# Four transformer layers on one core: where the softmax of the two 32-wide attentions is divided by its row sums

## The chip, the cores and the metric

The kernel runs on one core of one Trainium2 chip. The metric is the device time of one execution in microseconds; lower is better. Engines are named as in the profile: PE is TensorE (PEld its weight loads), DVE VectorE, ACT ScalarE, POOL GpSimd, SP the engine that issues DMAs.

## The reference

Four pre-norm transformer layers follow each other on x of 4 batches x 512 rows x 512 columns, each `x = x + attention(layernorm(x))`, then `x = x + feed_forward(layernorm(x))`. The change touches the attentions of the first two layers, 16 heads 32 wide, causal:

```python

q = (x @ Wq).reshape(B, S, N_KV, GROUP, HEAD_DIM)
k = (x @ Wk).reshape(B, S, N_KV, HEAD_DIM)
v = (x @ Wv).reshape(B, S, N_KV, HEAD_DIM)
scores = jnp.einsum('bqkgd,bskd->bkgqs', q, k) * scale
scores = jnp.where(causal, jnp.finfo(scores.dtype).min, scores)
attn = jax.nn.softmax(scores, axis=-1)
...

AV = jnp.einsum('bhqk,bhkd->bhqd', A, V)
return AV @ Wo + bo
```

The first five lines and the mask are layer 0 (4 key/value heads, each shared by 4 query heads, no biases; the heads go through V and Wo as in layer 1); the last two are layer 1, with 16 key/value heads, its own second layernorm weights ln_g and ln_b, and biases bq, bk, bv, bo. Everything is float32.

## The kernel before

Both attentions are made by one function, `attention32` (line 502), called as a0 (one chunk of keys, `split_y` true) and a1 (four chunks, biased). x stays in SBUF for the whole kernel. A float32 product that needs full precision is made of three (`product`, lines 101 to 103) from high and low halves; one that doesn't is `plain` (line 108).

Work is cut into 16 units an attention: 4 batches b times 4 groups u of 4 heads (128 rows of features). A unit has three chunks j: the scores of query tile 3 (512 wide), of tiles 2 and 0 (384 + 128), of tile 1 (256). For each chunk n:

- S: TensorE makes the scores of four heads into banks 0 to 3, in two halves (line 950).
- `low`: VectorE adds the causal mask, writes P and takes the row minimum (line 867); this frees the score banks.
- `exp`: ScalarE, in place, with the row sums in `total` (line 788).
- `rec`: VectorE takes the inverse of the sums (line 873) and multiplies heads 0 and 1 of P by them (line 878); GpSimd multiplies heads 2 and 3 (line 715).
- PT: TensorE turns 128x128 tiles of P, four to a group, ten groups a unit (line 961), into banks 4 and 5; ScalarE copies each group out (line 795).
- PV: TensorE multiplies by V into bank 6 (line 976). Behind the tenth group ScalarE copies O (line 800), and GpSimd passes it on to OT: in a0 as a high and a low half (lines 735, 737), in a1 as a copy (line 739).

Between these stand "pieces", each into bank 7: projections Q, K, V (VT and V in a0) of this or the next batch, T (transposes of the normalised x for the next batch), Y (the output product of the batch before). A Q or K piece is read by ScalarE (high half) and then VectorE (low half, lines 851, 848); a Y piece is added to x by VectorE (line 895); T is copied by ScalarE, cast by GpSimd (line 708), its low half made by VectorE (line 833).

The order is a list written out by hand, `ORDER`. Every engine walks it and does its own kinds, in that order, so a wait of one engine holds all that stands behind it on that engine. Iteration n has: `low` (n+2, 0 and 1), `rec` (n+1), `low` (n+2, 2 and 3), then two halves, each of up to two PT, the PV of two groups before, two `exp` of chunk n+2, and in the first half the near piece; then the first half of S for chunk n+3, the far piece, the second half of S. Near and far pieces go by (u, j); for j = 1 the near piece is Y for u = 0 and 1, Q for u = 2, and for u = 3 Q in a0 and V in a1; in the first batch there is no Y, in the last no piece of a next batch. For j = 0 the far piece is a K in a1, except for u = 2, where it is a T in both. Banks are handed over by counting semaphores: a job waits until the job before it in its bank has been read.

## Time and profile before

| what | us |
|---|---|
| median of 3 runs | 3340.04 (3339.21 to 3345.2) |
| the profiled execution | 3342.46 |
| its span, first to last instruction | 3340.6 |
| TensorE busy in it | 2978.2 (89%) |
| VectorE busy | 1976.6 (59%) |
| ScalarE busy | 1556.4 (47%) |
| GpSimd busy | 1030.8 (31%) |

The page gives busy time by engine and the costliest groups of instructions. A group's row has the line, the engine, the operation, written tile <- read tiles, shapes and count, then its busy time, the mean duration of one in ns, and the idle time of the engine just before, with what ended it. The names `a_...` cover both attentions here and two later ones; the line tells them apart. Matmuls overlap, so the time that one takes of TensorE is busy time through count, not its mean duration. "PEclk" is the mean clock granted to TensorE, 1.00 for 2.4 GHz and 0.50 for 1.2 GHz.

a0 lies in about the first 376 us, a1 between about 795 and 1245 us. The stretches 36:366 and 803:1232 hold most of them.

### The profile page before, as it was taken

The numbers are of one execution on the slowest core, as the hardware profiler recorded it, in microseconds if no ns is written. First come the engines' busy times: TensorE is split into PE (matmuls) and PEld (weight loads), VectorE is DVE, ScalarE is ACT, GpSimd is POOL, SyncE is SP. The second block draws the span as 40 slices with busy tenths as digits, with TensorE's granted clock in tenths as the row PEclk, the third lists the DMA queues.
The fourth block names the chain that finished last, engine by engine and source line by source line (L and its number), as shares of the span: only waits on it lengthen the run. The fifth ranks groups of instructions, "written<-read, shape, count | busy, mean of one in ns | idle before, by whom it ended". The sixth has DMA issues, their size and how long they took to land. (4 is left out here: it accounts for less than half of the span.)

```text
span 3340.6 us, 46876 instructions
## 1 busy us (share of the span) xinstructions
PE 2978.2 (89%) x16388; PEld 2252.2 (67%) x16388; DVE 1976.6 (59%) x5344; ACT 1556.4 (47%) x3606; POOL 1030.8 (31%) x1150
## 2 busy tenths in 40 slices
PE   6999799997999986968879958998599999989999
PEld 4777578885666754445567747774377777778887
DVE  5666587775565555332657767664677787742121
ACT  5777565664666653142322354444455555531000
POOL 3565332232454440000057651000123233322222
PEclk9999899998999996988889989999799999999999
DMA  2000311011000003203200110004000000020000
GB/s 89 2 2 1 114 31 33 29 32 67 1 1 1 1 17 116 76 30 117 70 0 7 44 61 1 1 1 143 12 1 1 1 1 1 1 104 13 13 13 13
DMA packets 65872, 105.51 MB, mean 32 GB/s; under 512 B 9315, under 2 KB 29795, under 8 KB 65509
## 3 DMA queue, kind: packets, MB, share of 16 engines
q1 hardware_dynamic: 65222, 102.41, 8.9%
q8 instruction: 132, 2.16, 0.3%
q14 instruction: 102, 0.84, 0.1%
q0 software_dynamic: 416, 0.10, 0.0%
HBM read 89.75 MB, written 12.85 MB: 31 GB/s over the span
## 5 line engine op out<-in xcount | busy, mean ns | idle before, releaser
L715 POOL TENSOR_SCALAR a_P<-a_P,a_rec 128x512 f32<-128x512 f32 (+3 forms) x256 | 301.0, 1187 | 349.3 <-DVE a_rec L873 349.3
L403 ACT ACTIVATE tree_value<-tree_bit,table_lut,tree_step 128x256 f32<-128x256 uint8 x496 | 275.3, 595 | 144.7 <-DVE tree_value L417 72.2
L417 DVE COPY_PREDICATED tree_value<-tree_bit,tree_value 128x256 f32<-128x256 uint8 x434 | 234.4, 545 | 138.6 <-ACT tree_value L403 110.3
L788 ACT ACTIVATE a_P<-a_P,a_low 128x384 f32<-128x384 f32 (+3 forms) x512 | 281.7, 557 | 25.7 <-DVE a_low L867 25.3
L101 PE MATMUL bank<-f_xT_hi,f_w_hi 128*128 128x512 f32 (+1 forms) x704 | 275.9, 392 | 13.8 <-DVE f_w_lo L1215 13.8
L102 PE MATMUL bank<-f_xT_hi,f_w_lo 128*128 128x512 f32 (+1 forms) x704 | 275.6, 392 | 0.0
L103 PE MATMUL bank<-f_xT_lo,f_w_hi 128*128 128x512 f32 (+1 forms) x704 | 275.3, 391 | 0.0
L1137 POOL CAST f_h_hi<-f_sg 128x512 fp32r<-128x512 f32 (+1 forms) x88 | 84.7, 963 | 587.0 <-DVE f_sg L1237 298.0
L867 DVE CUSTOM_DVE_ANT_0 a_P<-bank,a_causal 128x384 f32<-128x384 f32 (+3 forms) x512 | 222.9, 482 | 61.9 <-PE bank L950 61.4
L795 ACT ACTIVATE a_PT<-bank 128x512 f32<-128x512 f32 x320 | 174.1, 594 | 83.3 <-PE bank L961 82.6
L1237 DVE TENSOR_TENSOR f_sg<-bank,f_sg 128x512 f32<-128x512 f32 (+1 forms) x44 | 30.4, 691 | 269.8 <-PE bank L103 269.8
L961 PE MATMUL bank<-ident,a_P 128*128 128x128 f32 x1280 | 179.2, 285 | 10.9 <-issue 6.0
L961 PEld LDWEIGHTS bank<-ident,a_P 128*128 128x128 f32 x1280 | 147.2, 145 | 42.4 <-issue 30.9
L2402 ACT ACTIVATE a_PT<-bank 128x512 f32<-128x512 f32 x112 | 61.7, 595 | 223.2 <-PE bank L2675 223.2
L1173 ACT ACTIVATE f_sg<-bank 128x512 f32<-128x512 f32 (+1 forms) x44 | 26.3, 598 | 296.6 <-PE bank L103 296.6
L101 PEld LDWEIGHTS bank<-f_xT_hi,f_w_hi 128*128 128x128 f32 (+1 forms) x704 | 132.3, 188 | 42.9 <-issue 14.2
L103 PEld LDWEIGHTS bank<-f_xT_lo,f_w_hi 128*128 128x128 f32 (+1 forms) x704 | 132.3, 188 | 28.8
L102 PEld LDWEIGHTS bank<-f_xT_hi,f_w_lo 128*128 128x128 f32 (+1 forms) x704 | 132.3, 188 | 28.7
L101 PE MATMUL bank<-f_w_hi,f_h_hi 128*128 128x512 f32 (+1 forms) x352 | 140.5, 399 | 11.2 <-POOL f_h_lo L1139 11.1
L2389 ACT ACTIVATE a_P<-bank,a_nm,a_qs 128x256 f32<-128x256 f32 (+1 forms) x256 | 134.4, 544 | 20.7 <-DVE a_nm L2539 20.6
L103 PE MATMUL bank<-f_w_lo,f_h_hi 128*128 128x512 f32 (+1 forms) x352 | 138.5, 394 | 0.0
L102 PE MATMUL bank<-f_w_hi,f_h_lo 128*128 128x512 f32 (+1 forms) x352 | 138.4, 393 | 0.0
(467 smaller groups left out, 7908.2 us busy)
## 6 DMA issues: line engine op xcount, KB each, us to landing
f_w_raw<-in_f_w SPq DMA_DIRECT2D x11, 768.0 KB, 12.9
f_w_raw<-table_w SPq DMA_DIRECT2D x11, 768.0 KB, 11.7
tree_idx<-in_f_idx SPq DMA_DIRECT2D x62, 128.0 KB, 2.1
table_w<-tree_value SPq DMA_DIRECT2D x62, 128.0 KB, 1.7
x_res<-in_x SPq DMA_DIRECT2D x4, 1024.0 KB, 11.3
m_piece<-in_m_wq SPq DMA_DIRECT2D x2, 2048.0 KB, 12.1
m_piece<-in_m_wo SPq DMA_DIRECT2D x2, 2048.0 KB, 8.7
m_piece<-in_m_w_gate SPq DMA_DIRECT2D x2, 2048.0 KB, 10.6
```

What stands on the lines that cost most here:

```text
L101: pe.matmul(out, w[0], x[0], start=first, stop=False, skip_group_check=True)
L102: pe.matmul(out, w[1], x[0], start=False, stop=False, skip_group_check=True)
L103: return pe.matmul(out, w[0], x[1], start=False, stop=last, skip_group_check=True)
L403: act.activation(prog.tree_value[(h + to) % 4][:, :], prog.tree_bit[h % 2][0][:, :], ACT.Identity, bias=prog.table_lut[:, 2 * k:2 * k + 1] ...
L417: dve.copy_predicated(prog.tree_value[(h + keep) % 4][:, :], prog.tree_bit[h % 2][bit][:, :], prog.tree_value[(h + other) % 4][:, :]).then ...
L715: last = pool.tensor_scalar(Pr[j][:, g, col:col + n], Pr[j][:, g, col:col + n], rec[:, j, i, g:g + 1], None, ALU.mult)
L788: last = act.activation(Pr[j][:, k, col:col + n], Pr[j][:, k, col:col + n], ACT.Exp, bias=low[:, j, i, k:k + 1], scale=-1.0, accum_out=tot ...
L795: act.activation(PT[at % NPT][:, :], ps[J.bank(key)][:, :], ACT.Copy).then_inc(J.frees(key), 1)
L867: last = dve.tensor_tensor_reduce(out=Pr[j][:, k, col:col + n], in0=ps[J.bank(source)][:, col:col + n], in1=causal[:, T - n:T], scale=-sca ...
L961: last = pe.transpose(ps[J.bank(key)][:, g * P:(g + 1) * P], Pr[j][:, g, col + kt * P:col + (kt + 1) * P], prog.ident[:, :])
L1137: pool.tensor_copy(h[i % 2][0][0:n, :], sg[i % 2][0:n, :]).then_inc(c_hi.sem, 1)
L2389: e = act.activation(Pr[i][:, hh, lo:2 * P], ps[3 + j][:, h2 * 2 * P + lo:(h2 + 1) * 2 * P], ACT.Exp, bias=small["nm"][:, i, hh:hh + 1], s ...
```

## The change

P stays as the exponentials leave it. The inverse sums of a whole unit, four query tiles times four heads, sit side by side in `rec` [128, 16] and are taken once a unit (`rec` at the second chunk of the unit). TensorE turns them (RT, into bank 7), VectorE copies the result to `turned` [16, 128]. With a constant selector `spread` [16, 512], TensorE makes four `plain` products (SP, into bank 7), which give each row of O its inverse sum; ScalarE copies them to SBUF in place of copying O, and VectorE multiplies O from its bank with them, in place. The ORDER has RT in the second chunk ahead of the near piece, and SP in the next unit's first chunk ahead of its PT; `low` of heads 2 and 3 now comes behind PT, PV and O. VectorE takes over the copies of the PT groups 1, 4 and 7 of each ten. The low half of xT goes from VectorE to GpSimd. In a1 OT becomes a ring of five tiles that O is written to directly. What else stood in the entry `rec` (statistics, normalising, roots, the bias onto x) is now in an entry `side`, at the same place. Cut to its core:

```diff
-        OT_raw = prog.sb(name + "_OT", [P, DC, T], F32)
+        OT_raw = prog.sb(name + "_OT", [P, RING, T], F32)
...
-    O = [prog.sb(f"{name}_O{i}", [P, T], F32) for i in range(2)]
+    O = [prog.sb(f"{name}_O{i}", [P, T], F32) for i in range(2)] if split_y else None
     low = prog.sb(name + "_low", [P, 3, 2, G], F32)
-    total = prog.sb(name + "_total", [P, 3, 2, G], F32)
-    rec = prog.sb(name + "_rec", [P, 3, 2, G], F32)
+    total = prog.sb(name + "_total", [P, 2, TT * G], F32)
+    rec = prog.sb(name + "_rec", [P, 2, TT * G], F32)
+    turned = prog.sb(name + "_turned", [TT * G, P], F32)
+    spread = prog.sb(name + "_spread", [TT * G, TT * P], F32)
...
+        if j == 1:
+            ORDER.append((("rec", m, 0), 0))
         if n + 1 < CHUNKS:
-            ORDER.append((("rec", n + 1, 0), 0))
-        if n and n + 2 < CHUNKS:
-            ORDER += [(("low", n + 2, 2), 0), (("low", n + 2, 3), 0)]
+            ORDER.append((("side", n + 1, 0), 0))
         for half in range(2):
             some = groups[2 * half:2 * half + 2]
...
+            if j == 0 and half == 0 and m:
+                ORDER.append((("SP", m - 1, 0), PIECE))
             ORDER += [(("PT", i, 0), PT_BANK + i % 2) for i in some]
             ORDER += [(("PV", i - 2, 0), 0) for i in some if i >= 2]
             if j == 0 and half == 0 and m:
                 ORDER.append((("O", m - 1, 0), O_BANK))
                 if UNITS[m - 1][1] > 1:
                     ORDER.append((("OT", m - 1, 0), 0))
...
+            if half == 0 and n and n + 2 < CHUNKS:
+                ORDER += [(("low", n + 2, 2), 0), (("low", n + 2, 3), 0)]
             if n + 2 < CHUNKS:
                 ORDER += [(("exp", n + 2, g), 0) for g in (2 * half, 2 * half + 1)]
+            if j == 1 and half == 0:
+                ORDER.append((("RT", m, 0), PIECE))
             if half == 0:
                 ORDER += [(piece, PIECE) for piece in near]
...
+    ORDER += [(("SP", NU - 1, 0), PIECE)] + [(("PV", i, 0), 0) for i in (len(GROUPS) - 2, len(GROUPS) - 1)]
+    ORDER += [(("O", NU - 1, 0), O_BANK), (("OT", NU - 1, 0), 0)]
...
+    OWN = (1, 4, 7)
...
+    def inverse(m):
+        return O[m % 2][:, :] if split_y else OT_raw[:, m % RING, :]
...
                     pool.tensor_copy(xT[0][:, k, :], xT_raw[:, k, :]).then_inc(c_xhi.sem, 1)
-                elif kind == "rec":
+                    pool.wait_ge(*c_xhi(0, n + 1))
+                    pool.tensor_tensor(xT[1][:, k, :], xT_raw[:, k, :], xT[0][:, k, :].bitcast(F32), ALU.subtract).then_inc(c_xlo.sem, 1)
+                elif kind == "side":
                     j = at % 3
-                    pool.wait_ge(*c_rec(0, at + 1))
-                    for g in range(G // 2, G):
-                        for i, (col, qt) in enumerate(PARTS[j]):
-                            n = (qt + 1) * P
-                            last = pool.tensor_scalar(Pr[j][:, g, col:col + n], Pr[j][:, g, col:col + n], rec[:, j, i, g:g + 1], None, ALU.mult)
-                    last.then_inc(c_scaled.sem, 1)
...
-                        pool.tensor_copy(OT_raw[:, c, :], O[at % 2][:, :]).then_inc(c_ot.sem, 1)
...
-                                              accum_out=total[:, j, i, k:k + 1])
+                                              accum_out=total[:, at // 3 % 2, qt * G + k:qt * G + k + 1])
                     last.then_inc(c_exp.sem, 1)
-                elif kind == "PT":
+                elif kind == "PT" and at % PER not in OWN:
                     act.wait_ge(*full(key))
                     if at >= NPT:
                         act.wait_ge(*used(at - NPT))
                     act.activation(PT[at % NPT][:, :], ps[J.bank(key)][:, :], ACT.Copy).then_inc(J.frees(key), 1)
...
+                elif kind == "SP":
                     act.wait_ge(*full(key))
-                    if at >= 2:
-                        act.wait_ge(*c_ot(0, at - 1))
-                    act.activation(O[at % 2][:, :], ps[J.bank(key)][:, :], ACT.Copy).then_inc(J.frees(key), 1)
+                    if split_y:
+                        if at >= 2:
+                            act.wait_ge(*c_ot(0, at - 1))
+                    elif at >= RING:
+                        act.wait_ge(*full(("Y", UNITS[at - RING][0], TT - 1)))
+                    act.activation(inverse(at), ps[J.bank(key)][:, :], ACT.Copy).then_inc(J.frees(key), 1)
...
-                    dve.wait_ge(*c_xhi(0, n + 1))
-                    dve.tensor_tensor(xT[1][:, k, :], xT_raw[:, k, :], xT[0][:, k, :].bitcast(F32), ALU.subtract).then_inc(c_xlo.sem, 1)
...
+                elif kind == "PT" and at % PER in OWN:
+                    dve.wait_ge(*full(key))
+                    if at >= NPT:
+                        dve.wait_ge(*used(at - NPT))
+                    dve.tensor_copy(PT[at % NPT][:, :], ps[J.bank(key)][:, :]).then_inc(J.frees(key), 1)
                 elif kind == "rec":
-                    j, parts = at % 3, len(PARTS[at % 3])
-                    dve.wait_ge(*c_exp(0, G * (at + 1)))
-                    dve.reciprocal(rec[:, j, 0:parts, :], total[:, j, 0:parts, :]).then_inc(c_rec.sem, 1)
-                    dve.wait_ge(*c_rec(0, at + 1))
-                    for g in range(G // 2):
-                        for i, (col, qt) in enumerate(PARTS[j]):
-                            n = (qt + 1) * P
-                            last = dve.tensor_scalar(Pr[j][:, g, col:col + n], Pr[j][:, g, col:col + n], rec[:, j, i, g:g + 1], None, ALU.mult)
-                    last.then_inc(c_own.sem, 1)
+                    dve.wait_ge(*c_exp(0, 3 * G * (at + 1)))
+                    dve.reciprocal(rec[:, at % 2, :], total[:, at % 2, :]).then_inc(c_rec.sem, 1)
+                elif kind == "RT":
+                    dve.wait_ge(*full(key))
+                    dve.tensor_copy(turned[:, :], ps[J.bank(key)][0:TT * G, 0:P]).then_inc(J.frees(key), 1)
+                elif kind == "O":
+                    dve.wait_ge(*read(("SP", at, 0)))
+                    dve.wait_ge(*full(key))
+                    dve.tensor_tensor(inverse(at), ps[J.bank(key)][:, :], inverse(at), ALU.mult).then_inc(J.frees(key), 1)
...
-                        pe.wait_ge(*c_own(0, 3 * m + j + 1))
-                        pe.wait_ge(*c_scaled(0, 3 * m + j + 1))
+                        pe.wait_ge(*c_exp(0, G * (3 * m + j + 1)))
...
+                elif kind == "RT":
+                    pe.wait_ge(*c_rec(0, at + 1))
+                    pe.wait_ge(*vacant(key))
+                    pe.transpose(ps[J.bank(key)][0:TT * G, 0:P], rec[:, at % 2, :], prog.ident[:, :]).then_inc(J.fills(key), 1)
+                elif kind == "SP":
+                    if at == 0:
+                        pe.wait_ge(*c_const(0, 16 * n_const))
+                    pe.wait_ge(*read(("RT", at, 0)))
+                    pe.wait_ge(*vacant(key))
+                    for qt in range(TT):
+                        last = plain(pe, ps[J.bank(key)][:, qt * P:(qt + 1) * P], spread[:, qt * P:(qt + 1) * P], turned[:, :], True, True)
+                    last.then_inc(J.fills(key), 1)
...
-                            last = plain(pe, ps[J.bank(key)][:, :], OT_raw[:, c, k * P:(k + 1) * P], wo_raw[:, c, :], c == 0, c == DC - 1)
+                            last = plain(pe, ps[J.bank(key)][:, :], OT_raw[:, (DC * at + c) % RING, k * P:(k + 1) * P], wo_raw[:, c, :],
+                                         c == 0, c == DC - 1)
...
-    spread = np.zeros((P, TT, P), f)
-    sums[:, 0, TT:] = 1
+    spread = np.zeros((TT, 4, TT, P), f)
     for qt in range(TT):
-        sums[:, qt, qt] = 1
         for g in range(4):
-            spread[32 * g + qt, qt, 32 * g:32 * g + 32] = 1
+            spread[qt, g, qt, 32 * g:32 * g + 32] = 1
```

## Rows read from the trace of the kernel before

**Rows 1.** Busy by stretch: width; PE, PEld, DVE, ACT, POOL us (count); clock, DMA share, GB/s.
```profile
36.00:366.00 330.00, 299.64 (x3137) 230.89 (x3135) 218.21 (x766) 253.60 (x726) 195.29 (x180) 0.96 0.01 2
...
803.00:1232.00 429.00, 400.51 (x3403) 287.93 (x3402) 242.57 (x805) 273.98 (x748) 197.24 (x193) 0.96 0.01 1
```

**Rows 2.** TensorE's waits in 36:366: waiter, releaser, us in total, times, longest.
```profile
PE bank L950 <- DVE a_low L867: 18.2, 10, 4.5
...
PE bank L961 <- issue: 2.1, 3, 0.8
```

**Rows 3.** TensorE's waits in 803:1232.
```profile
PE bank L950 <- DVE a_low L867: 10.6, 7, 2.1
...
PE bank L101 <- DVE a_Q_lo L848: 6.2, 3, 3.1
...
PE bank L961 <- issue: 3.9, 4, 1.8
```

**Rows 4.** Groups by line in 36:366, VectorE and GpSimd: busy us, mean ns, idle before.
```profile
L878 DVE TENSOR_SCALAR a_P<-a_P,a_rec 128x512 f32<-128x512 f32 (+3 forms) x128 | 62.4, 539 | 1.7
...
L715 POOL TENSOR_SCALAR a_P<-a_P,a_rec 128x512 f32<-128x512 f32 (+3 forms) x128 | 150.7, 1188 | 131.0 <-DVE a_rec L873 131.0
...
L737 POOL TENSOR_TENSOR a_OT_lo<-a_O,a_OT_hi 128x512 fp32r<-128x512 f32 x16 | 22.4, 1400 | 1.4
...
L708 POOL CAST a_xT_hi<-a_xT_raw 128x512 fp32r<-128x512 f32 x12 | 7.2, 609 | 15.4 <-ACT a_xT_raw L759 15.4
```

**Rows 5.** Groups by line and shape: a0's transposes, fourth attention's products, VectorE's bank reads.
```profile
L961 PE MATMUL bank<-ident,a_P 128*128 128x128 f32 x640 | 89.7, 285 | 4.9 <-issue 2.1 <-DVE a_Q_lo L851 1.5 <-ACT a_PT L795 0.8
...
L2667 PE MATMUL bank<-a_KT,a_QT 128*128 128x128 f32 x120 | 17.0, 287 | 4.3 <-ACT a_QT L2379 4.3
...
L895 DVE TENSOR_TENSOR x_res<-x_res,bank 128x512 f32<-128x512 f32 x32 | 21.9, 686 | 57.3 <-PE bank L108 30.2 <-PE bank L103 27.1
...
L2467 DVE COPY a_k<-bank 128x64 f32<-128x64 f32 x16 | 3.5, 218 | 1.7 <-issue 1.1 <-ACT a_V L2367 0.5
```

**Rows 6.** Timeline, a0 unit, second chunk: start us, us, engine, work, idle before.
```profile
154.19 0.69 DVE L867 CUSTOM_DVE_ANT_0 a_P<-bank,a_causal 128x512 f32<-128x512 f32 x1 [0.69 <-PE bank L950]
...
154.80 0.69 DVE L867 CUSTOM_DVE_ANT_0 a_P<-bank,a_causal 128x512 f32<-128x512 f32 x1
...
155.56 0.50 PE L101 MATMUL bank<-a_wo_hi,a_OT_hi 128*128 128x512 f32 x1
```

**Rows 7.** Timeline, a1 unit, second chunk.
```profile
973.56 0.75 DVE L848 SCALAR_TENSOR_TENSOR a_K_lo<-bank,a_aff,a_K_hi 128x512 fp32r<-128x512 f32 x1 [4.53 <-ACT a_K_hi L779]
...
975.22 3.70 PE L108 MATMUL bank<-a_wo,a_OT 128*128 128x512 f32 x8
```

**Rows 8.** Timeline, a0, unit u = 2.
```profile
176.64 1.07 PE L961 MATMUL bank<-ident,a_P 128*128 128x128 f32 x8 [0.84 <-issue]
...
179.27 0.50 PE L101 MATMUL bank<-a_xT_hi,a_wq_hi 128*128 128x512 f32 x1 [0.99 <-DVE a_xT_lo L833]
```

**Rows 9.** Timeline, a0, behind a K piece.
```profile
190.28 1.09 PE L961 MATMUL bank<-ident,a_P 128*128 128x128 f32 x8
...
190.45 0.69 DVE L851 TENSOR_TENSOR a_K_lo<-bank,a_K_hi 128x512 fp32r<-128x512 f32 x1 [1.22 <-ACT a_K_hi L781]
```

**Rows 10.** Timeline at a0's start, VectorE and TensorE.
```profile
39.10 0.18 DVE L873 RECIPROCAL a_rec<-a_total 128x4 f32<-128x4 f32 x1 [4.01 <-ACT a_P L788]
...
42.15 0.58 PE L950 MATMUL bank<-a_K_hi,a_Q_hi 32*128 32x256 f32 x2 [4.46 <-DVE a_low L867]
```

**Rows 11.** Timeline of TensorE, two waits for `low` in a0.
```profile
208.90 0.39 PE L950 MATMUL bank<-a_K_hi,a_Q_hi 32*128 32x256 f32 x2 [1.39 <-DVE a_low L867]
...
339.43 0.50 PE L950 MATMUL bank<-a_K_hi,a_Q_hi 32*128 32x512 f32 x2 [2.32 <-DVE a_low L867]
```

**Rows 12.** Busy time by stretch behind those two waits.
```profile
339.40:344.40 5.00, 4.97 (x38) 3.81 (x38) 3.25 (x11) 3.73 (x11) 4.12 (x5) 0.66 0.02 3
...
208.90:213.00 4.10, 4.00 (x38) 3.15 (x39) 2.59 (x10) 4.10 (x15) 2.40 (x3) 1.00 0.02 4
```

More of the change, by code:

```diff
@@ L634, in attention32 @@
                 jobs.append((("O", m, 0), O_BANK))
-        elif kind not in ("low", "exp", "rec", "O", "OT"):
+        elif kind not in ("low", "exp", "rec", "side", "O", "OT"):
             jobs.append(((kind, at, k), BANK[(kind, at, k)]))
@@ L645, in attention32 @@
     c_xn, c_shift, c_rec = (prog.count(n) for n in ("xn", "shift", "rec"))
+    OWN = (1, 4, 7)
     c_whi, c_wlo, c_xhi, c_xlo = (prog.count(n) for n in ("w_hi", "w_lo", "xT_hi", "xT_lo"))
-    c_qk, c_exp, c_scaled, c_own, c_pv = (prog.count(n) for n in ("qk_hi", "p_exp", "p_scaled", "p_scaled_dve", "pv"))
+    c_qk, c_exp, c_pv = (prog.count(n) for n in ("qk_hi", "p_exp", "pv"))
     c_ot_hi, c_ot = (prog.count(n) for n in ("ot_hi", "ot_lo"))
-    n_const = 1 + (5 if biased else 0)
+    n_const = 2 + (5 if biased else 0)
+    def inverse(m):
+        return O[m % 2][:, :] if split_y else OT_raw[:, m % RING, :]
     NQK = DC + KC
@@ L669, in _ @@
                     sp.dma_start(causal[:, :], ins["c_causal"]).then_inc(c_const.sem, 16)
+                    sp.dma_start(spread[:, :], ins["c_spread"]).then_inc(c_const.sem, 16)
                     if biased:
@@ L728, in _ @@
                             pool.tensor_tensor(x[:, t * D:(t + 1) * D], x[:, t * D:(t + 1) * D], bo[:, :], ALU.add).then_inc(c_shift.sem, 1)
-                elif kind == "OT":
+                elif kind == "OT" and split_y:
                     b, c = UNITS[at]
@@ L830, in _ @@
                 if kind == "T":
-                    n = at * DC + k
-                    dve.wait_ge(*c_xhi(0, n + 1))
-                    dve.tensor_tensor(xT[1][:, k, :], xT_raw[:, k, :], xT[0][:, k, :].bitcast(F32), ALU.subtract).then_inc(c_xlo.sem, 1)
-                    if n == DC - 1:
+                    if at == 0 and k == DC - 1:
                         for i, (w, raw, _) in enumerate(WEIGHTS):
@@ L978, in _ @@
                     last.then_inc(J.fills(out) if at % PER == PER - 1 else c_pv.sem, 1)
+                elif kind == "RT":
[10 more added lines that the diff above has]
+                    last.then_inc(J.fills(key), 1)
                 elif kind == "Y":
                     if k == 0:
-                        pe.wait_ge(*c_ot(0, DC * (at + 1)))
-                        if at == 0 and split_y:
-                            pe.wait_ge(*c_wlo(0, 4))
+                        if split_y:
+                            pe.wait_ge(*c_ot(0, DC * (at + 1)))
+                            if at == 0:
+                                pe.wait_ge(*c_wlo(0, 4))
+                        else:
+                            pe.wait_ge(*read(("O", DC * at + DC - 1, 0)))
                     pe.wait_ge(*vacant(key))
@@ L1008, in attention32 @@
     c_exp.advance(G * CHUNKS)
-    c_rec.advance(CHUNKS)
-    c_scaled.advance(CHUNKS)
-    c_own.advance(CHUNKS)
+    c_rec.advance(NU)
     c_pv.advance((PER - 1) * NU)
-    c_ot.advance(NU)
+    c_ot.advance(NU if split_y else 0)
     c_ot_hi.advance(NU if split_y else 0)
```

19 lines of the change are left out of this document (9 added, 10 removed).

## The prediction

> **What bounds the kernel now.** Start with the busy time of each engine in the two stretches that the change touches, the steady parts of the attentions a0 and a1 [rows 1]. TensorE is busy for 299.6 of 330 us and 400.5 of 429 us; ScalarE, the next, for 253.6 and 274.0. So look at TensorE's waits, not at the engine that does the scaling. They are 30.4 us in a0 and 28.5 us in a1 (330.0 less 299.6, 429.0 less 400.5), and the list of waits says what ended them: mostly VectorE's `low`, which frees the score banks [rows 2], and in a1 also `a_Q_lo` [rows 3]. The clock adds some: a mean grant of 0.96 over 759 us is 0.04 x 759 = 30 us of full-speed work lost [rows 1]. The most that the change can give back is thus 59 us of waits and 30 us of clock. Whatever is put onto TensorE, or into its way, counts in full.
>
> The scaling itself is large on its engines, 62.4 us of VectorE and 150.7 us of GpSimd in a0 [rows 4], a1 alike. But no wait of TensorE names GpSimd's scaling, and at the transposes it waits only 2.1 and 3.9 us with no releaser ("issue") [rows 2, 3]. The scaling hurts through VectorE's queue: `low` stands behind it.
>
> **TensorE's new work.** Each of the 32 units (16 an attention) gets one transpose of the inverse sums (RT) and four plain float32 products of 128 columns (SP), eight records, since a float32 product shows as two. A transpose costs 89.7/640 = 0.14 us of TensorE, a plain 128x128 record 17.0/120 = 0.142 us in the fourth attention [rows 5]. That is 0.14 + 8 x 0.142 = 1.28 us a unit, 41 us for 32. Nothing hides it, since TensorE leads. I take these rows because they have the same shape and operand width; SP contracts over 16 rows only, which I don't count as a gain. Below, 8 x 0.11 us (pure streaming) would give 33 us; above, 0.28 us a record, the duration of one that overlaps nothing, 77 us.
>
> **The wait behind RT.** RT uses bank 7, as every projection piece does, and VectorE empties it. In order, VectorE has at that place: two `low`, the reciprocal, the copy of PT group 4 (now its own), two more `low`, the copy of `turned`. TensorE has PT, PT, PV, PV, RT, and then the near piece, which needs bank 7 back. I time it on one unit of a0 [rows 6]. TensorE starts the near piece at 155.56. VectorE ends its second `low` at 155.4 (154.80 + 0.69, less the 0.08 by which it overlaps the next); reciprocal 0.2, PT copy 0.65 (it costs what other full-bank reads of VectorE cost, 0.686 [rows 5]), two `low` 1.22 + 0.08, copy of `turned` about 0.22 (a 64-column copy took 218 ns [rows 5]): 157.8. The near piece starts then, 2.2 us later; 0.14 of it is RT itself, so 2.1 us of wait. The `low` can't come earlier: VectorE waited for the scores before the first of them.
>
> In a1 a K piece lies between the two score halves, and `a_K_lo` stands ahead of the `low`: it begins at 973.56, the near piece at 975.22 [rows 7]. The same sum from 974.2 on (four `low` 2.44, reciprocal 0.2, PT copy 0.65, `turned` 0.22 and some 0.2 between) gives 977.9: 2.6 us later, 2.5 without RT. This holds for the units u = 0, 1 and 3 that have a near piece in their second chunk. Over four batches (none for u = 0, 1 of the first batch and for u = 2, 3 of the last) that is 9 units an attention: 9 x 2.1 + 9 x 2.5 = 41 us.
>
> For u = 2 TensorE loses now 0.84 us ahead of PT and 0.99 us for `a_xT_lo` [rows 8]. The low half of xT moves to GpSimd, where a cast takes 0.61 us and such a subtraction 1.40 us [rows 4]. Freed of the scaling, GpSimd does the third tile while the fourth is still being turned; the fourth is copied at about 176.0 (TensorE's last scores end at 175.8, 176.64 less 0.84, and the tile went ahead of them), so its low half is there near 178.0. RT's wait, by the sum above from 175.8, ends near 178.4, against 179.27 now. I count 1.0 us of wait there, six times, 6 us, and the old 1.83 us among what goes. Together 47 us. The bounds: 0 if something else held TensorE just as long, and some 3.5 us a unit if VectorE comes late.
>
> **The wait ahead of SP.** SP takes bank 7 too, right behind the last scores, and finds the piece before it unread. After a K piece, `a_K_hi` and `a_K_lo` end at 191.1, where TensorE would be ready at 190.28 [rows 9]: 0.9 us. After Y, V or T pieces I put 0.2 to 0.5. Over 28 units 6 to 25 us; I take 10, near the lower end, as both readers have less to do. The rest of SP (ScalarE's copy takes the place of the O copy, VectorE multiplies O) hides behind PT, PT, PV, PV.
>
> **What goes.** With the scaling, VectorE's `low` comes 1.0 to 1.5 us earlier in each chunk. The waits for it were mostly 1.4 to 2.3 us, and these are what [rows 2, 3] hold. In a1 the statistics of the next batch no longer stand behind a scaling that shares its time with GpSimd, so `a_Q_lo` should be in time. At the start of an attention VectorE stood in the reciprocal until all exponentials of the first chunk were done (4.01 us), and TensorE 4.46 us behind it [rows 10]; this goes. What stays I put at 8 us: the last O's way to the output product, and small ones behind ScalarE. Of 59 us I take off 51. ScalarE gives 48 PT copies an attention to VectorE; it is nowhere first except in the last two units, where this is within those 51.
>
> **The clock.** A wait of 2.32 us [rows 11] was followed by 5.0 us at a mean grant of 0.66, that is, some 3.4 us of them at the lower level, 1.2 GHz; one of 1.39 us was not followed by any [rows 12]. One such fall costs 0.34 x 5.0 = 1.7 us. Old falls: of 30 us I take 20 off with their waits. New ones: 18 waits of 2.1 to 2.5 us, at 1.7 us and 7 in 10 of them, 21 us. Net 1 us; I write 2 for shorter falls behind SP.
> The Trainium skill, "TensorE: Matmul & The Clock Gate", section "A second HAM failure mode: psum-queue depth-cycling", says that a TensorE which idles shortly but often between groups, because banks cycle, swings between the two clock levels. It speaks against this change, which adds just such pauses; by it all 18 waits would be followed by a fall, 9 us more than my sum. The trace agrees for the wait of 2.32 us, not for the one of 1.39 us.
>
> **The rest.** For the first xT of an attention GpSimd now makes four casts and four subtractions in a row, 4 x (0.61 + 1.40) = 8.0 us. VectorE's split of the first weights runs beside it and hides most; I take 1 us an attention, 2 us. Without that cover the subtractions would cost 5.6 us. The `spread` load (16 partitions) is a further issue on SyncE's queue ahead of the K weights, whose cast waits for ScalarE anyway: nothing, at most 0.5 us. Dropping GpSimd's copy into OT in a1 saves well under 1 us, once, at the end.
>
> **Sum.** 41 + 47 + 10 - 51 + 2 + 2 = +51 us. The profiled execution took 3342.5 us (its span is 3340.6), the median of the runs is 3340.0, 2.4 less; so 3342.5 + 51 - 2.4 = 3391 us.
>
> **Rivals.**
> First, the forecast: TensorE pays for RT and SP and waits for bank 7. 3391 us, chance 0.62.
> Second, faster: RT's wait is hidden. The place is bank 7 in the second chunk of each unit. If VectorE, freed of the scaling, reached the `turned` copy before TensorE needs the bank, 47 us and the 21 us of new clock falls drop out: +51 - 68 = -17, 3323 us. It turns faster once the mean wait behind RT is below about 0.6 us (each 1 us of it is 24 us, and with its fall more). For it speaks that VectorE is busy for 218 of 330 us only; against it that its queue is in order and that four `low` and a full-bank copy stand there between the scores and the copy. Chance 0.13.
> Third, worse: every wait is followed by a fall (+9), SP's wait is at its 25 us (+15), and a record costs 0.18 us (+10). 3425 us, chance 0.13.
> Fourth, the terms cancel: the waits are about 1 us a unit (-24) and no new fall follows them (-21), so +6: 3344 us. Chance 0.07. That the change does not do what it says is no rival of weight (0.05 for odd outcomes between): the P scaling is gone from the code, and GpSimd must fall by about 300 us in the two attentions.
>
> The range that holds 8 in 10 reaches from 3345, near the fourth case, to 3425, the third. A measurement of this kernel can tell about 0.2%, 6.7 us, from no change. Faster 0.13, within it 0.06, slower 0.81.
>
> **What would show it.** In the changed profile: no groups for the P scaling and GpSimd down by some 270 us; TensorE waits for `low` nearly gone; in their place waits ahead of the pieces (the product helper's first line) ended by VectorE's copy of `turned`, some 2 us each, about 18 of them, and some ahead of SP ended by `a_K_lo`; VectorE and ScalarE less busy in a longer stage; the granted clock at or under 0.96. The a0 stretch should be about 25 us longer, a1 about 25. The prediction is wrong if no wait stands behind RT, or if SP's eight records take under 0.6 us.

## The result, and the profile after

The changed kernel takes 3416.83 us (median of 4 runs, 3416.26 to 3426.38), the kernel before, beside it, 3340.07 us: a ratio of 1.0233, 95% interval 1.0213 to 1.0254. It is 77 us slower. The forecast was +51 us with a range up to 3425 us. The direction and the mechanism held; the size was 26 us short, of which 3 us lie between the profiled executions (73.9 us apart) and the medians (76.8).

The head of the page after (share of the span; before, PE had 2978.2 us, DVE 1976.6, ACT 1556.4 and POOL 1030.8):

```profile
span 3414.5 us, 47016 instructions
PE 3023.5 (89%) x16676; PEld 2288.8 (67%) x16676; DVE 1913.8 (56%) x5152; ACT 1508.5 (44%) x3510; POOL 766.0 (22%) x910
```

Three engines work less, GpSimd by 265 us. TensorE works 45 us more, and it is the one that counts.

To see where the 73.9 us of the two profiled spans lie (3414.5 less 3340.6), cut each attention from a fixed event to a fixed event: a0 from 12.9 us to the first normalising of the feed-forward part behind it, a1 from its own first normalising to the first operation of the next stage. Before:

```profile
12.90:380.50 367.60, 329.34 (x3248) 253.65 (x3248) 235.23 (x792) 262.10 (x736) 198.43 (x184) 0.95 0.04 15
782.21:1255.00 472.79, 423.99 (x3464) 301.28 (x3464) 261.44 (x833) 284.39 (x759) 204.61 (x203) 0.94 0.05 15
```

After (columns as in [rows 1]):

```profile
12.90:416.80 403.90, 351.33 (x3392) 269.82 (x3392) 206.07 (x695) 238.24 (x688) 67.60 (x72) 0.96 0.04 13
822.34:1330.80 508.46, 442.76 (x3608) 315.66 (x3608) 227.16 (x737) 260.08 (x711) 69.42 (x75) 0.94 0.05 14
```

a0 is 36.3 us longer, a1 35.7, the rest 2. In both together TensorE is busy 40.8 us more (22.0 and 18.8) and idle 31.2 us more (52.57 less 38.26, and 65.70 less 48.80). The mean grant hardly moves: summed over slices of 1 us, what the grant lacks of 1.00 is 48.7 us in the two stages before and 46.0 us after. (This sum is called the lost clock below.)

The idle time by what ended it, a0 after (waiter, releaser, us in total, times, longest):

```profile
PE bank L101 <- DVE a_turned L890: 18.8, 12, 1.8
...
PE bank L101 <- POOL a_xT_lo L727: 8.6, 1, 8.6
PE bank L108 <- ACT a_xT_raw L769: 3.4, 3, 3.0
PE bank L108 <- ACT a_V L781: 2.9, 3, 1.0
...
PE bank L108 <- DVE a_K_lo L861: 2.8, 3, 0.9
PE bank L967 <- DVE a_low L877: 2.4, 4, 0.8
```

and a1 after:

```profile
PE bank L101 <- POOL a_xT_lo L727: 16.9, 1, 16.9
PE bank L108 <- DVE a_turned L890: 10.3, 6, 1.8
PE bank L101 <- DVE a_turned L890: 8.5, 6, 1.8
...
PE bank L998 <- DVE a_rec L887: 5.0, 11, 0.5
PE bank L108 <- ACT a_xT_raw L767: 4.0, 3, 3.2
PE bank L967 <- DVE a_low L877: 2.4, 4, 0.8
```

L877 is the `low` that was L867 in [rows 2, 3]: 18.2 and 10.6 us became 2.4 and 2.4, and a1's 6.2 us for `a_Q_lo` are gone. In their place stand 24 waits for the copy of `turned`, 37.6 us, and the waits of the plain products for whoever has to empty bank 7 ahead of SP. The new work itself, by groups in a0 (line, engine, work, count, busy us, mean ns, idle before):

```profile
L108 PE MATMUL bank<-a_turned,a_spread 16*128 16x128 f32 x128 | 18.0, 279 | 10.4 <-ACT a_xT_raw L769 3.4 <-ACT a_V L781 2.9 <-DVE a_K_lo L861 2.8
...
L998 PE MATMUL bank<-ident,a_rec 128*16 128x128 f32 x16 | 4.4, 277 | 1.0
L890 DVE COPY a_turned<-bank 16x128 f32<-16x128 f32 x16 | 4.4, 273 | 0.0
```

One unit of a0 after, second chunk, answers to [rows 6]:

```profile
119.22 0.69 DVE L877 CUSTOM_DVE_ANT_0 a_P<-bank,a_causal 128x512 f32<-128x512 f32 x1 [4.51 <-PE bank L967]
...
120.44 0.25 DVE L887 RECIPROCAL a_rec<-a_total 128x16 f32<-128x16 f32 x1
120.61 0.63 DVE L884 COPY a_PT<-bank 128x512 f32<-128x512 f32 x1
...
120.75 0.28 PE L998 MATMUL bank<-ident,a_rec 128*16 128x128 f32 x1
121.15 0.68 DVE L877 CUSTOM_DVE_ANT_0 a_P<-bank,a_causal 128x512 f32<-128x512 f32 x1
...
122.36 0.27 DVE L890 COPY a_turned<-bank 16x128 f32<-16x128 f32 x1
...
122.78 0.47 PE L101 MATMUL bank<-a_xT_hi,a_wq_hi 128*128 128x512 f32 x1 [1.76 <-DVE a_turned L890]
```

RT starts at 120.75, 0.31 us behind the start of the reciprocal, and bank 7 then stays taken through a full-bank copy and two `low` until its 16 rows are copied. This is the order that the prediction laid out, and TensorE stands behind it for 1.76 us.

### The profile page after: what moved, and what is told of

The parts are those of the page before. It is cut to its first block and busy times, and to the rows that moved or that the text cites. A ratio compares the mean times of both kernels' runs of the same rounds, so it can differ in the third digit from the quotient of the medians.

```text
span 3414.5 us, 47016 instructions
## 1 busy us (share of the span) xinstructions
PE 3023.5 (89%) x16676; PEld 2288.8 (67%) x16676; DVE 1913.8 (56%) x5152; ACT 1508.5 (44%) x3510; POOL 766.0 (22%) x910
## 5 line engine op out<-in xcount | busy, mean ns | idle before, releaser
L877 DVE CUSTOM_DVE_ANT_0 a_P<-bank,a_causal 128x384 f32<-128x384 f32 (+3 forms) x512 | 222.1, 486 | 83.0 <-PE bank L967 83.0
L805 ACT ACTIVATE a_PT<-bank 128x512 f32<-128x512 f32 x224 | 126.7, 595 | 130.7 <-PE bank L977 130.4
L2432 ACT ACTIVATE a_PT<-bank 128x512 f32<-128x512 f32 x112 | 61.6, 595 | 223.3 <-PE bank L2705 223.3
L101 PE MATMUL bank<-a_xT_hi,a_wq_hi 128*128 128x512 f32 x192 | 82.3, 428 | 43.0 <-POOL a_xT_lo L727 25.5
## 6 DMA issues: line engine op xcount, KB each, us to landing
m_piece<-in_m_wq SPq DMA_DIRECT2D x2, 2048.0 KB, 11.9
```

The costliest lines, as they stand in the source:

```text
L101: pe.matmul(out, w[0], x[0], start=first, stop=False, skip_group_check=True)
L805: act.activation(PT[at % NPT][:, :], ps[J.bank(key)][:, :], ACT.Copy).then_inc(J.frees(key), 1)
L877: last = dve.tensor_tensor_reduce(out=Pr[j][:, k, col:col + n], in0=ps[J.bank(source)][:, col:col + n], in1=causal[:, T - n:T], scale=-sca ...
L2432: act.activation(PT[G % 2][:, j, :], ps[5 + j][:, :], ACT.Copy).then_inc(J.frees(("PT", G, j)), 1)
```

## Experiments

Ratios are against the kernel before, run beside each on the same chip; 0.001 is 3.3 us. All diffs are against the changed kernel unless said otherwise.

**RT behind the near piece.** Is the order in bank 7 what costs, and does its whole price come back?

```diff
-            if j == 1 and half == 0:
+            if j == 1 and half == 1:
                 ORDER.append((("RT", m, 0), PIECE))
```

> The turning of the inverse sums (RT) moves behind the near piece, into the second half of the chunk; nothing else changes. Theory A (bank 7 held by RT costs the wait): in the changed kernel TensorE waits 37.6 us for the copy of turned and 5.0 us for the reciprocal; both are hidden here, RT then waits for the near piece's reader instead, about 0.5 us a unit at most. Expected 3417 - 43 + 8 = 3382 us, with the waits for a_turned under 5 us. Rival B (TensorE would wait as long for something else, VectorE's or ScalarE's queue): within 5 us of 3417. Rival C (each wait also costs a fall of the clock): 3417 - 60 or below, about 3355.

3365.31 us, ratio 1.0084 (1.0067 to 1.0101), 50 us less than the change. The waits for `a_turned` and `a_rec` are gone from the list; `a_PT` by VectorE grew from 4.0 to 7.0 us and `a_xT_lo` by 1.9 us. So of the 42.6 us of waits behind and ahead of RT only about 5 came back elsewhere. This settles the second rival against: a hidden RT wait would have given nothing here. The gain is larger than theory A's (3382 us) and smaller than theory C's (3355): in the profile the two stages shrank by 47.0 us, of which 37.2 are idle time and 9.7 busy time, with 5 us less lost clock.

**Only VectorE's order.** RT stays, its copy goes ahead of the last two `low`.

```diff
+            if j == 1 and half == 0:
+                ORDER.append((("RT", m, 0), PIECE))
             if half == 0 and n and n + 2 < CHUNKS:
                 ORDER += [(("low", n + 2, 2), 0), (("low", n + 2, 3), 0)]
```

(in VectorE's order; the old entry behind them is dropped there)

> Only VectorE's order changes: the copy of turned stands ahead of the last two lows of the chunk instead of behind them. TensorE's order is that of the changed kernel. Theory A (VectorE's queue ahead of the copy makes the wait): two lows, 1.0 to 1.3 us, leave the wait in front of 24 near pieces, about 28 us less wait: 3390 us, the waits for a_turned down from 37.6 to about 10 us. What the two lows lose, TensorE's next scores have a near piece as cover, so under 3 us come back. Rival B (the hand-over itself, transposing and passing bank 7, makes the wait): over 3410 us.

3385.43 us, 1.0144 (1.0129 to 1.0159): 30 us less. The waits for `a_turned` in a0 fell from 18.8 to 6.0 us:

```profile
PE bank L101 <- DVE a_turned L890: 6.0, 12, 0.5
```

1.57 us a wait became 0.5, about what the two `low` take (1.2 us, 121.15 to 122.36 above). VectorE's place in its queue, not its load, makes the wait; it was busy for only 206 of 404 us.

**All PT copies on ScalarE**, as before the change (`OWN = (1, 4, 7)` becomes `OWN = ()`).

> The changed kernel, but ScalarE copies all groups of PT, as before the change; VectorE copies none. Theory A (VectorE's order between the scores and the copy of turned makes RT's wait): the copy of PT group 4, some 0.65 us, no longer stands ahead of the copy of turned, so each of the 24 waits is some 0.6 us shorter: 3417 - 15 = 3402 us, and VectorE's own PT waits (4 us) go. Theory B (ScalarE now stands in the way: with three copies of 0.5 to 0.6 us more a unit ahead of its exponentials, VectorE's inverse sums come later and new waits for ScalarE's PT appear): within 5 us of 3417, or slower.

3388.58 us, 1.0146 (1.0131 to 1.0161): 28 us less, twice what was expected. The waits behave as theory A says, 0.6 us less each, 37.6 us down to 23.2, VectorE's own PT waits gone, only 0.6 us more for ScalarE's. That makes 18 us. In the profile the two attentions shrank by 22.2 us (10.3 and 11.9) and the stages that were not touched by 5; that share of the gain lies outside the edit, and I take it for chance of the execution, which is not shown. The other 5 us are busy time of TensorE, and not the clock (the lost clock is 46.8 us, against 46.0). What they are stays open.

**First low halves back on VectorE.** Is GpSimd's part at the start the price it looks like?

```diff
                 if kind == "T":
+                    if at == 0:
+                        dve.wait_ge(*c_xhi(0, k + 1))
+                        dve.tensor_tensor(xT[1][:, k, :], xT_raw[:, k, :], xT[0][:, k, :].bitcast(F32), ALU.subtract).then_inc(c_xlo.sem, 1)
```

(and GpSimd leaves them out for the first batch)

> The low halves of the first batch's xT go back to VectorE in both attentions, the other batches stay on GpSimd. Theory A: GpSimd's subtractions stand beside VectorE's split of the weights and the two hold each other up; the first product of a0 began 3.5 us later and that of a1 about 7 us later than before, so 3417 - 10 = 3407 us. Rival B (my estimate in the forecast, 1 us each): 3415 us. Rival C (the start is absorbed in a later wait): 3417.

3405.67 us, 1.0212 (1.0191 to 1.0233). Against the change that is 7 us less by the ratios, and the two intervals overlap, so by its time alone this run doesn't show a gain. Its profiled execution is the slowest of its four (3418.79 us), with 10 us more lost clock than the change's. The waits are plain, though: TensorE's two start waits, 8.6 and 16.9 us for `a_xT_lo`, became 14.9 us for `a_wq_lo`, 10.6 us less. With RT and SP moved (below), the same edit gave 3329.07 against 3341.51 us, 12 us, and there the intervals are apart.

**No scaling at all.** RT, SP and the multiplication are left out; VectorE copies O as it is, so the output is that of unnormalised attentions.

> RT, SP and the multiplication are left out, so the output of both attentions is not divided by its row sums; VectorE copies O. Shows what the other half of the change is worth. Theory A: 46 us of new work on TensorE, 43 us behind RT and 17 us ahead of SP go, 106 us: 3417 - 106 = 3311 us, 29 us under before. Rival B (part of the waits returns elsewhere, lows and PT copies): 3325 to 3335 us. Rival C (the scaling was hidden anyway and its removal alone gives nothing): 3340 us or over.

3298.41 us, 0.9881 (0.9866 to 0.9896), 40 us less than the kernel before and below all three expectations. The other parts of the change are still in: the first low halves on GpSimd, three PT copies of ten on VectorE. Beside them, taking the P scaling away gives 40 us. The stages (columns as in [rows 1]) say of what:

```profile
12.90:358.20 345.30, 316.86 (x3248) 244.68 (x3248) 202.30 (x681) 228.96 (x672) 67.38 (x72) 0.98 0.05 16
761.23:1213.70 452.47, 409.75 (x3464) 291.22 (x3464) 223.36 (x721) 250.84 (x695) 69.65 (x75) 0.96 0.05 16
```

TensorE's idle time is 71.2 us, only 15.9 less than the 87.1 of the kernel before, and the busy time of the same number of records is 26.7 us less, with 24.9 us of lost clock against 48.7. The sum had counted 51 us of waits and 20 us of clock: here the clock's share came, and the waits' did not. And the new way of scaling, with its waits and falls, costs 3416.8 less 3298.4 = 118 us.

**SP twice.** The eight records are issued again (`for qt in list(range(TT)) * 2`).

> The changed kernel with SP's four products made twice, the same values over each other. Theory A (TensorE is the engine that all of SP counts on, in full): 32 x 1.15 = 37 us more than the changed kernel, 3452 us on a chip where before takes 3338. Rival B (SP lies partly beside other engines' work that ends last): under 20 us more.

3466.65 us, 1.0368 (1.0352 to 1.0384), 45 us over the change (0.0135 x 3340), 1.4 us a unit. That is more than the 37.3 us that SP's records take in the change; the second set took 34.8 us (36.0 and 36.1 us for all, less 18.0 and 19.3). The clock is the likely surplus, not shown apart: in a0 the mean grant fell from 0.96 to 0.93, and the lost clock of both stages rose from 46.0 to 76.8 us. a0 in this run:

```profile
12.90:438.90 426.00, 375.63 (x3520) 292.19 (x3520) 206.79 (x696) 238.94 (x688) 67.63 (x72) 0.93 0.04 13
```

**RT late and SP early.** SP moves from the head of the next unit to chunk 2 of its own, where bank 7 has long been read (in a1's u = 1 behind the near piece).

```diff
-            if j == 0 and half == 0 and m:
-                ORDER.append((("SP", m - 1, 0), PIECE))
+            if j == 2 and half == (0 if split_y or u != 1 else 1):
+                ORDER.append((("SP", m, 0), PIECE))
```

> RT behind the near piece as in the run that moved it alone, and SP moved ahead of the PT of its own unit's third chunk, far from the piece before it in bank 7 (for u = 1 of a1 behind the near piece, since its ring slot is read only there). Theory A: of 17 us of waits ahead of SP about 12 go, the ones behind K, T and V pieces: 12 us under the run with RT late alone, 3353 us against 3338 for the kernel before. Rival B (ScalarE copies the spread sums ahead of two PT copies, which then come late; the near piece waits for it): no gain, 3365 us or more.

3341.51 us, 0.9996 (0.9985 to 1.0007), the time of the kernel before. Against RT late alone it is 0.0088 or 29 us less (each side of it known to 4 to 6 us), where 12 were expected. This surplus led to the next two runs.

**SP early alone**, RT as in the change.

> Only SP is moved: from the head of the next unit to chunk 2 of its own unit (in a1's u = 1 behind the near piece); RT stays ahead of the near piece, with its waits. Theory A (the waits ahead of SP and the clock falls behind them add to everything else): the same move took about 29 us off when RT was already moved, 17 us of it waits and the rest clock, so here 3417 - 29 = 3388 us, with the mean grant of the a0 window up from 0.96 to 0.98. Theory B (the clock gain came only from having no short waits left at all; with RT's waits of up to 1.8 us still there the clock stays at 0.96): only the 17 us of waits go, 3400 us. Theory C (SP closer behind RT lengthens RT's wait, since the turned copy is now needed for SP one chunk later, with VectorE in order): above 3405 us.

3390.74 us, 1.0154 (1.0137 to 1.0171), 26 us less than the change: theory A by the time. But not by its reason: the grant of a0 is 0.95, not 0.98. The lost clock of the two stages is 48.2 us, no less than the change's 46.0. Nor are the waits as forecast: idle time fell by 8.5 us only, all in a0, since in a1 others came (2.6 us for `x_res`, 1.9 for `a_K_lo`, 1.8 for the ScalarE copy of the sums). The two stages shrank by 23.5 us, 15.0 of them busy time. Two things show in the traces.

The first is the clock, and where it falls. In the change, from 40 to 400 us, slices of 1 us show seven falls, and each begins some 1 us behind a wait ahead of SP, six of them of 0.93 to 0.99 us, the first of 2.97. Of the 12 waits of 1.06 to 1.76 us behind RT in this stretch none was followed by one (in a1 three were, at 1087, 1145 and 1210 us; and there two falls began behind waits as short as 0.55 us, at 898, and 0.41 us, at 1162). The wait at 132.98 and the one at 146.26:

```profile
132.98 1.12 PE L108 MATMUL bank<-a_turned,a_spread 16*128 16x128 f32 x8 [0.98 <-ACT a_V L781]
...
146.26 0.47 PE L101 MATMUL bank<-a_wo_hi,a_OT_hi 128*128 128x512 f32 x1 [1.76 <-DVE a_turned L890]
```

and the stretches behind them (the grant is the third number from the right):

```profile
134.00:136.00 2.00, 2.00 (x25) 1.49 (x24) 1.78 (x7) 2.00 (x7) 0.00 (x0) 0.70 0.00 0
136.00:138.00 2.00, 2.00 (x12) 1.46 (x5) 1.43 (x6) 0.74 (x4) 0.69 (x2) 0.50 0.00 0
...
146.00:150.00 4.00, 3.74 (x20) 3.10 (x20) 0.80 (x2) 0.26 (x1) 0.00 (x0) 1.00 0.00 0
```

0.50 is the lower of the two levels, 1.2 GHz. The seven cost 11.9 us (the sum of what the slices lack of 1.00), 1.7 us each. With SP early alone, the falls that go with SP's waits are gone, and of the 11 waits behind RT between 116 and 338 us now four are followed by a fall (at 117, 161, 250 and 338 us). With both moved, no fall is left between 50 and 340 us. The rule that a longer wait decides, on which the prediction stood, is not borne out: the same waits behind RT were followed by falls in one version and by none in the other. SP's shape does not do it, since SP without a wait is followed by none. The trace of the kernel before had it already. The prediction took the wait of 1.39 us at 208.90 [rows 11], which no fall followed; two others of the same length and kind, and the stretch behind the first, are these:

```profile
125.44 0.39 PE L950 MATMUL bank<-a_K_hi,a_Q_hi 32*128 32x256 f32 x2 [1.39 <-DVE a_low L867]
...
291.66 0.39 PE L950 MATMUL bank<-a_K_hi,a_Q_hi 32*128 32x256 f32 x2 [1.39 <-DVE a_low L867]
...
125.00:130.00 5.00, 4.56 (x34) 3.45 (x35) 3.48 (x15) 4.33 (x13) 3.30 (x4) 0.66 0.00 0
```

A fall followed each of them (the second from 293 to 297 us), and none followed a wait of 1.80 us at 65.27.

The second is that SP, placed behind scores with no wait, runs between them. RT late and SP early, one unit:

```profile
201.59 0.37 PE L108 MATMUL bank<-a_turned,a_spread 16*128 16x128 f32 x1
201.75 0.23 PE L967 MATMUL bank<-a_K_hi,a_Q_hi 32*128 32x128 f32 x2
201.80 0.27 PE L108 MATMUL bank<-a_turned,a_spread 16*128 16x128 f32 x1
201.81 0.28 PE L967 MATMUL bank<-a_K_hi,a_Q_lo 32*128 32x128 f32 x2
201.92 0.27 PE L108 MATMUL bank<-a_turned,a_spread 16*128 16x128 f32 x1
201.92 0.28 PE L967 MATMUL bank<-a_K_lo,a_Q_hi 32*128 32x128 f32 x2
202.03 0.72 PE L108 MATMUL bank<-a_turned,a_spread 16*128 16x128 f32 x5
202.68 0.55 PE L977 MATMUL bank<-ident,a_P 128*128 128x128 f32 x3
```

From the last score group (201.75) to the transposes (202.68) it is 0.93 us, against 0.39 us in the version without scaling (196.25 to 196.64): SP costs 0.54 us there, and 1.05 us in the change, where it follows a wait. 24 of the 32 units show this. The Trainium skill, "TensorEngine Tiling (Array Packing)", section "Key Properties", says that different tiles of the array can load weights and multiply in parallel. The trace agrees with it: records of 16 and of 32 rows start in turns, 0.11 us and less apart, and with 128 rows (the next run) none do.

**SP over 128 rows.** The run with RT late and SP early, with `turned` and `spread` padded with zeros to 128 rows, so that SP takes the whole array.

```diff
-    turned = prog.sb(name + "_turned", [TT * G, P], F32)
-    spread = prog.sb(name + "_spread", [TT * G, TT * P], F32)
+    turned = prog.sb(name + "_turned", [P, P], F32)
+    spread = prog.sb(name + "_spread", [P, TT * P], F32)
```

> The run with RT late and SP early, but SP contracts over all 128 rows (the turned sums and the selector are padded with zeros), with the same eight records of 128 columns. In that run SP's records of 16 rows lie between score records of 32 rows in 24 of 32 units: the first SP record starts 0.16 us before the last score group, and from there to the transposes 0.93 us go by, against 0.39 us in the kernel without SP. So SP costs 0.54 us there, where it cost 1.05 us in the changed kernel. Theory A (TensorE works on the score products and on SP at once, since both take few rows): with 128 rows that is gone, SP costs 1.05 us again, 24 x 0.52 = 12 us more: 3341.5 + 12 = 3354 us, and no SP record starts before the last score. Theory B (the gain of the move beyond its waits was the clock alone): the clock and the time stay, 3342 us.

3340.17 us, 0.9996 (0.9986 to 1.0006). The two halves of theory A part here. The records do as it says:

```profile
204.09 0.23 PE L970 MATMUL bank<-a_K_hi,a_Q_hi 32*128 32x128 f32 x2
204.15 0.28 PE L970 MATMUL bank<-a_K_hi,a_Q_lo 32*128 32x128 f32 x2
204.26 0.28 PE L970 MATMUL bank<-a_K_lo,a_Q_hi 32*128 32x128 f32 x2
204.47 1.16 PE L108 MATMUL bank<-a_turned,a_spread 128*128 128x128 f32 x8
205.47 0.71 PE L980 MATMUL bank<-ident,a_P 128*128 128x128 f32 x5
```

No SP record lies between scores, and the way from the last score group to the transposes is 1.38 us, 0.45 more. But the time is the same within 5 us; a cost of 12 us, as theory A had it, is excluded. Four units of steady work took 82.65 us against 81.41 (101.02 to 183.67, 99.76 to 181.17), 0.31 us a unit, 7 us for 24 units, and even that does not show in the medians. In the two profiled executions the stages differ by 6.4 us (842.5 against 836.1), with 3.5 us less lost clock in the slower, but executions of one of these kernels lie up to 13 us apart. The overlap is shown, its worth is not: at most some 5 us.

**All moves, and SP stacked.** The moves of RT, SP and the first low halves together:

> The former, and the first batch's low halves of xT on VectorE: all waits that the change added are taken away as far as the order allows, its 46 us of work on TensorE stay. Theory A (effects add): 10 us under the former, 3343 us, still about 0.2% above before, since 46 us of stream stand against about 39 us of waits gone. Rival B: the effects overlap, and it stays over 3350 us.

3329.07 us, 0.9959 (0.9945 to 0.9974), 14 us under what was expected. Then SP as four rounded (fp32r) products, the high and low halves of the turned sums stacked in rows 0 to 31 and 32 to 63 against a selector that has its ones twice:

```diff
-                    dve.tensor_copy(turned[:, :], ps[J.bank(key)][0:TT * G, 0:P]).then_inc(J.frees(key), 1)
+                    dve.tensor_copy(turned[0:32, :], ps[J.bank(key)][0:32, 0:P]).then_inc(c_turn.sem, 1)
+                    dve.wait_ge(*c_turn(0, at + 1))
+                    dve.tensor_tensor(turned[32:64, :], ps[J.bank(key)][0:32, 0:P], turned[0:32, :].bitcast(F32), ALU.subtract).then_inc(J.frees(key), 1)
```

> As the former, but SP's four float32 products become four single passes: turned holds a high half in rows 0 to 31 and a low half in rows 32 to 63, both fp32r, and the selector stands twice, so one pass of 64 rows adds them. Eight records become four. Theory A (SP's stream is on the path in full): SP falls from 1.15 to about 0.5 us a unit, 32 x 0.65 = 21 us: 3322 us, 16 us under before. Rival B (weight loads set SP's pace, 0.14 us a record): 32 x 0.55 = 18 us. Rival C (VectorE's second operation on the turned sums, 0.3 us, stands in the path): under 8 us gained.

3321.95 us, 0.9938 (0.9925 to 0.9951), 7 us below the one before it, not the 21 that half the records suggest. The trace has a reason: four records of 64 rows do not start before the last score and cost 0.59 us (from 198.43 to 199.41, less 0.39), as much as the eight of 16 rows that ran between the scores. Last, the same with all PT copies on ScalarE:

> The fastest version so far (RT late, SP early, first low halves on VectorE, SP as four rounded products with high and low rows stacked; 3322 us), and in addition ScalarE copies all groups of PT. Theory A (VectorE's PT copies are what TensorE still waits for, 4.6 + 3.6 us, and no wait for ScalarE takes their place, as in the run with only this edit): 3322 - 7 = 3315 us. Theory B (ScalarE's queue becomes the late one): TensorE's waits for ScalarE's PT grow from 4.6 us in all by as much as VectorE's go, 3320 us or above. If the scalar copies had a gain of their own behind RT's wait (the 28 us of the run with this edit alone are more than the 14 us of waits that it took), it would show here, too: below 3308 us.

3318.11 us, 0.9937 (0.9918 to 0.9956): no difference from the one before. These two beat both kernels, the one before by 0.6%.

## Why the prediction was right in kind and short in size

**The bound.** Right. Three engines lost work, TensorE got work, and the time followed TensorE: 40.8 us busy and 31.2 us idle make the 72.0 us of the two stages.

**The stream.** Forecast 41 us. SP's groups are 18.0 and 19.3 us (L108), RT's 4.4 and 4.4 (L998): 46 us (46.2 with RT as 32 x 0.277 = 8.9). A record is 0.14 us, as taken from [rows 5]; RT's one transpose takes 0.277 us, since it stands alone and its end is not covered, where the prediction used 0.14 of a stream. That contraction over 16 rows brings nothing holds for the length of a record (0.14 us), but in the moved version half of it lay beside the scores.

**Behind RT.** Forecast 47 us, measured 37.6 us for `a_turned` in exactly the 24 places named, and 5.0 us ahead of RT in a1, where TensorE waits for the reciprocal. The six of u = 2 are 1.06 us as forecast; the 18 others are 1.67 to 1.76 where 2.1 and 2.5 stood. The way was right all the same. In a0 it is 2.03 us from RT's start to the near piece (120.75 to 122.78) against 2.2 forecast, with 0.28 us of it RT's own and not 0.14; in a1 the 2.5 us (2.6 if the prediction's own times are subtracted exactly) are split into 0.46 ahead of RT, 0.28 of RT and 1.76 behind. RT and its waits together were forecast at 47 + 32 x 0.14 = 51.5 us and came to 42.6 + 8.9 = 51.5. The clock term behind them (18 waits, 21 us of new falls) was wrong: 3 falls came behind the 24 waits, all in a1, not 7 in 10. The 7 in 10 rested on one wait with a fall and one without. The prediction also read the section that it cites of the Trainium skill, "TensorE: Matmul & The Clock Gate", "A second HAM failure mode: psum-queue depth-cycling", as a fall behind each of the 18 waits. The section gives no such count, and the trace has 3. The swings between the two levels that it describes did occur, in a0 seven times behind the waits ahead of SP.

**Ahead of SP.** Forecast 10 us, measured 16.8. In a0 `a_K_lo` costs 0.93 us a time, as read from [rows 9], but V pieces cost 0.98 and not 0.2 to 0.5 (in a1 they cost 0.2), and in each attention one xT copy holds SP for 3 us: ScalarE has the exponentials of a whole chunk ahead of it. The bounds (6 to 25) held it; the value near the low end did not, and the clock falls that came with these waits were priced at nearly nothing.

**What goes.** The largest error. The forecast had 51 us of waits and 20 us of clock; by difference 37.6 us of old waits went (31.2 more idle, less 42.6, 16.8 and 9.4 new). The run without any scaling has 15.9 us less idle time than the kernel before; with the start's waits, which it also pays (9.4 us in the change), some 25 us of waits went in it, not 51. It still waits, in a0 4.7 us for VectorE's PT copies and 2.4 for `low`, in a1 5.1 and 2.4: behind a releaser that is taken away stands the next. The sum had left 8 us of 59 standing, where some 21 stayed, 4.0 of them for PT copies that had not been VectorE's before. The clock's 20 us were there to be had (24 us in the run without scaling), but in the change new falls took their place: in a0 seven falls before (40 to 366 us, 12.6 us of full-speed work lost) became seven after (40 to 400 us, 11.9 us); those behind `low` went, those behind SP came.

**The start.** Forecast 2 us, measured 9.4 (3.3 in a0, 6.1 in a1). "VectorE's split of the weights hides most" failed: the two engines held each other up, below.

Put together, the terms are 46.2 + 42.6 + 16.8 - 37.6 + 9.4 = 77.4 us, where the two stages grew by 72.0. The 5.4 us between are in the busy time, which grew by 40.8 and not by the 46.2 of the new groups: a group's time counts where records overlap each other or old work, and the lost clock, 2.7 us less than before, is in it too. What makes the rest was not measured. Against the forecast that is stream +5, behind RT -4, ahead of SP +7, old waits +13, start +7, and -7 for the clock and this overlap: +21 in the stages, where the whole forecast was 51.

**The rivals.** That RT's wait is hidden is refuted by its 24 waits and by the run with RT late. That the terms cancel had the waits at 1 us; they were 1.57 on average. (That case's sum, +6, gives 3346 us and not the 3344 written.) The "worse" case (3425) had SP's wait at 25 us, a fall behind every wait and a record of 0.18 us; measured are 16.8 us, 3 falls behind 24 waits, and 0.14 us. So it came near by a wrong way, as the old waits that stayed are in neither. The time lies between the forecast and this case.

## What to carry over

Before a product moves onto the engine that leads, ask which bank it borrows and who must empty it: here the products took 46 us and the waits for their bank 59, and moving two entries of the order list gave 79 us back by the ratios (1.0233 to 0.9996), the waits with their clock falls and more. Price a removal by the next releaser in line, not by the waits that bear the old name: a version with the whole step left out had 16 us less idle time where 51 us had been counted. And put a helper product where its bank has long been read, not at the head of a unit.

## What the hardware showed

**Short pauses and the clock.** Pauses of 0.93 to 0.99 us ahead of SP were each followed by some 4 us at a lower grant (0.70, 0.50, then back), those of up to 1.76 us behind RT in the same attention by none; with SP's pauses gone, four of RT's eleven were. In the kernel before, three equal pauses of 1.39 us were followed by a fall twice and once by none. In the version with RT late and SP early no pause between 95 and 330 us is over 0.32 us, and the grant there is 1.00. So a pause costs its own time and, where a fall follows, 1.7 us more, which for the pauses ahead of SP is more than the pause. I had priced falls by the length of a pause, and that does not decide it; what does, these runs don't show.

**GpSimd and VectorE with two inputs in SBUF hold each other up.** The start of a0 after:

```profile
18.00 1.27 POOL L727 TENSOR_TENSOR a_xT_lo<-a_xT_raw,a_xT_hi 128x512 fp32r<-128x512 f32 x1
...
19.74 2.29 DVE L847 TENSOR_TENSOR a_wq_lo<-a_wq_raw,a_wq_hi 128x2048 fp32r<-128x2048 f32 x1 [5.56 <-ACT a_wq_hi L756]
19.91 3.25 POOL L727 TENSOR_TENSOR a_xT_lo<-a_xT_raw,a_xT_hi 128x512 fp32r<-128x512 f32 x1
...
21.95 1.75 DVE L847 TENSOR_TENSOR a_wk_lo<-a_wk_raw,a_wk_hi 128x512 fp32r<-128x512 f32 x1
...
25.89 0.80 PE L101 MATMUL bank<-a_xT_hi,a_wq_hi 128*128 128x512 f32 x1 [8.62 <-POOL a_xT_lo L727]
```

The same subtraction takes GpSimd 1.27 us alone and 3.25 us beside VectorE's; VectorE's next one takes 1.75 us, where it took 0.68 before. The first product came at 22.36 us before and comes at 25.89 now. The Trainium skill, "SBUF — State Buffer", section "Who interferes with whom", says that a VectorE instruction with two inputs in SBUF contends with a GpSimd instruction that reads SBUF, and that the one blocks and doesn't share. The trace agrees: GpSimd's 3.25 us is its own 1.27 and nearly all of the 2.29 us of VectorE's that began before it.
